# Attention and four expert layers on one core: additions to the output placed later, two tiles fetched before the hand-over

## What is computed

```
x = x + layernorm(attention(layernorm(x)))        # causal linear attention, 16 heads of 8, relu on q and k
x = x + layernorm(ffn(layernorm(x)))              # 4 layers, each:
#   logits = x @ rw[l] + rb[l]; the best 2 of 4 experts, weights renormalised
#   xhat = (x - mean) / sqrt(var + eps)
#   y_e  = gelu((xhat * g[e] + b[e]) @ w1[e] + b1[e]) @ w2[e] + b2[e]
#   x    = sum over the two experts e of weight_e * (x + y_e)
```

## Time and profile before

| | |
|---|---|
| median of 3 runs | 1578.39 us (1576.26 to 1583.17) |
| profiled execution, its own time | 1576.51 us |
| its span | 1574.6 us |
| PE, DVE, ACT, POOL busy | 88%, 78%, 71%, 54% |
| mean granted TensorE clock | 0.95 of full speed |
| attention block | up to about 403 us |
| last layer's first `fin`, last `fin` | 1312.88 us, 1559.35 us |

### The profile page before, as it was taken

The page is one execution under the profiler, slowest core; times in us unless marked ns, Lnnn a source line. Parts: engine busy times, 40 slices in busy tenths (PEclk is TensorE's granted clock), DMA queues, the critical chain, the costliest instruction groups (busy, mean ns, idle before and its releaser), DMA issues.

```text
span 1574.6 us, 36962 instructions
## 1 busy us (share of the span) xinstructions
PE 1389.8 (88%) x11037; PEld 1086.1 (69%) x11037; DVE 1233.7 (78%) x3763; ACT 1117.9 (71%) x1979; POOL 850.5 (54%) x1535
## 2 busy tenths in 40 slices
PE   6999999998679998999899999989989998888991
PEld 4666566566557877777787777778877776776770
DVE  6988788887358888788888878888887888677782
ACT  4444344442467898878788888778988788899881
POOL 2246556677665565345355534445563346787456
PEclk9998898998689999999999999999999999999995
DMA  7964565641657877665787766668766757886642
GB/s 280 400 264 137 220 245 201 232 169 31 167 163 223 250 228 212 194 180 169 211 251 227 221 184 200 180 192 262 228 214 181 213 170 199 214 206 159 178 105 21
DMA packets 181109, 314.11 MB, mean 199 GB/s; under 512 B 37568, under 2 KB 117808, under 8 KB 180528
## 3 DMA queue, kind: packets, MB, share of 16 engines
q1 hardware_dynamic: 159408, 288.27, 58.3%
q0 software_dynamic: 21504, 23.48, 6.4%
HBM read 205.20 MB, written 113.72 MB: 203 GB/s over the span
## 4 chain that ended last, share of the span: by engine, by line
PE 36%; issue 13%; DVE 12%; ACT 9%; POOL 4%; POOLq 0%; ACTq 0%; DVEq 0%
PE ps_h L1835 5%; PE ps_h L1837 5%; PE ps_h L1836 5%; PE ps_q L1868 5%; PE ps_y L1849 4%; PE ps_y L1851 4%; PE ps_y L1850 4%; ACT xh L1382 3%; ACT hh L1404 3%; DVE row L1540 2%; PE ps_t L1822 1%; DVE pbn L1483 1%; DVE hl L1477 1%; DVE row L1514 1%; POOL out_dram L1321 1%
## 5 line engine op out<-in xcount | busy, mean ns | idle before, releaser
L1398 ACT ACTIVATE hg<-ps_h,bb 128x512 f32<-128x512 f32 x592 | 387.7, 686 | 158.1 <-PE ps_h L1837 156.5
L1477 DVE TENSOR_TENSOR hl<-hg,hh 128x1024 fp32r<-128x1024 f32 x296 | 360.6, 1219 | 164.4 <-ACT hh L1404 164.3
L1404 ACT ACTIVATE hh<-hg 128x1024 fp32r<-128x1024 f32 x296 | 313.4, 1059 | 2.4
L1312 POOL DMA_INDIRECT regions<-nrow,posi x192 | 226.6, 1180 | 85.3 <-issue 47.9
L1835 PE MATMUL ps_h<-xTh,w1b 128*128 128x512 f32 x592 | 255.7, 432 | 8.4 <-ACT hg L1398 6.8
L1837 PE MATMUL ps_h<-xTh,w1b 128*128 128x512 f32 x592 | 234.9, 397 | 0.0
L1849 PE MATMUL ps_y<-hh,w2b 128*128 128x512 f32 x592 | 234.3, 396 | 0.0
L1836 PE MATMUL ps_h<-xTl,w1b 128*128 128x512 f32 x592 | 234.3, 396 | 0.0
L1851 PE MATMUL ps_y<-hh,w2b 128*128 128x512 f32 x592 | 233.3, 394 | 0.0
L1850 PE MATMUL ps_y<-hl,w2b 128*128 128x512 f32 x592 | 232.2, 392 | 0.0
L1868 PE MATMUL ps_q<-ir,yb 128*128 128x140 f32 (+2 forms) x888 | 138.8, 288 | 66.4 <-DVE base L1583 42.2
(11 more groups left out here) (280 smaller groups left out, 2630.2 us busy)
## 6 DMA issues: line engine op xcount, KB each, us to landing
w1b<-w_split SPq DMA_DIRECT2D x148, 512.0 KB, 4.1
w2b<-w_split SPq DMA_DIRECT2D x148, 512.0 KB, 4.6
regions<-zero SPq DMA_DIRECT2D x14, 4326.0 KB, 24.6
row<-regions SPq DMA_DIRECT2D x84, 294.0 KB, 4.4
w_split<-wst SPq DMA_DIRECT2D x32, 512.0 KB, 5.1
wr<-in_L_ffn_w_dram SPq DMA_DIRECT2D x32, 256.0 KB, 4.8
regions<-regions SPq DMA_DIRECT2D x24, 294.0 KB, 4.3
x<-in_L_attn_x_dram SPq DMA_DIRECT2D x16, 256.0 KB, 3.1
```

The lines of the kernel that those rows point to most:

```text
L1312: g.indirect_dma_start(out=regions[layer % 2], out_offset=bass.IndirectOffsetOnAxis(ap=posi[r % 2][:, b:b + 1], axis=0), in_=nrow[r % 2][: ...
L1398: a.activation(hg[c // 2 % PAIRS][:, c % 2 * TILE:(c % 2 + 1) * TILE], ps_h[c % BANKS][:], ACT.Gelu, bias=bb[h % BBUFS][:, c % FC:c % FC + ...
L1404: a.activation(hh[j % PAIRS][:], hg[j % PAIRS][:], ACT.Identity).then_inc(hi, 1)
L1477: v.tensor_tensor(hl[n][:], hg[n][:], hh[n][:].bitcast(F32), ALU.subtract).then_inc(lo, 1)
```

## The change

Four edits.

1. The additions of a last-layer tile get the index ENDS 2(j-10) instead of ENDS 2(j-8) in GpSimd's loop.
2. The first two operations of `last_rstd` (variance plus epsilon, mean times -1) move from GpSimd to VectorE, as `last_variance`, right behind `last_stats`.
3. The rows of the first two units are fetched by SP inside the attention block, ahead of the last tile's store of `x1`; their two buffers move to the part of memory that both blocks share.
4. Behind the barrier GpSimd does `rstd(0)` and `rstd(1)` ahead of `a_place(13)`, VectorE does `stats(0)` and `stats(1)` ahead of its wait for GpSimd's constants, and the counts of tile 14 (`count` on TensorE, `first_counts` on ScalarE) come behind PE's second chunk and ScalarE's first two gelus.

```diff
+                def first_rows():
+                    sp.wait_ge(t_tab, 1)
+                    for q in range(2):
+                        sp.wait_ge(s_scat[q], ((EARLY_FROM - 1 - q) // 2 + 1) * NB * 16)
+                    for n in range(2):
+                        at = sp.value_load(tabi[0][0:1, n, 0:1], min_val=0, max_val=ROWS - TILE)
+                        sp.dma_start(row_first[n][:], regions[0][ds(at, TILE)].rearrange("(b p) w -> p b w", p=P)).then_inc(row_in[n], 16)
                 for t in range(NT):
+                    if t == NT - 1:
+                        first_rows()
                     sp.wait_ge(a_x1, t + 1)
...
-                for n in range(2):
-                    rows_in(n)
                 for h in range(2):
                     first_weights(h)
...
                 def last_rstd(m):
                     n = PLACE[m]
-                    pool.wait_ge(f_mv, n + 1)
+                    pool.wait_ge(f_ve, 2 * n + 2)
                     wait(pool, f_n, n)
-                    g.tensor_tensor(fve[:], fmv[:, :, 1], epsc[:], ALU.add).then_inc(f_ve, 1)
-                    g.tensor_scalar(fngm[:], fmv[:, :, 0], -1.0, None, ALU.mult)
-                    pool.wait_ge(f_ve, n + 1)
                     g.tensor_tensor(frs[:], fve[:], half[:], ALU.pow).then_inc(f_rs, 1)
...
-                a_place(pool, NT - 3)
                 g.memset(oh[:, NB, :], 0.0)
...
                 pool.wait_ge(s_ir, 1)
+                rstd(0)
+                rstd(1)
+                a_place(pool, NT - 3)
                 a_choose(pool, NT - 2)
-                for n in range(3):
-                    rstd(n)
+                rstd(2)
                 a_rows_out(pool, NT - 3, range(NB))
...
+                    m = ENDS.get(2 * (j - 10))
                     if last_layer(m):
                         add_to_output(m)
                     m = ENDS.get(2 * (j - 7))
...
-                first_counts(NT - 2)
                 normed(0)
                 x_high(0)
                 normed(1)
                 gelu(0)
                 gelu(1)
+                first_counts(NT - 2)
...
+                def last_variance(m):
+                    n = PLACE[m]
+                    dve.wait_ge(f_mv, n + 1)
+                    wait(dve, f_nm, n)
+                    v.tensor_tensor(fve[:], fmv[:, :, 1], epsc[:], ALU.add).then_inc(f_ve, 1)
+                    v.tensor_scalar(fngm[:], fmv[:, :, 0], -1.0, None, ALU.mult).then_inc(f_ve, 1)
...
+                stats(0)
+                stats(1)
                 dve.wait_ge(s_ir, 1)
                 v.memset(sel[:], 0.0)
                 chained(v.tensor_scalar(tile_at[:], tiles[:, 0:LATE], float(TILE), None, ALU.mult))
-                stats(0)
-                stats(1)
                 x_rest(0)
...
                         if last_layer(n):
                             last_stats(n)
+                            last_variance(n)
...
-                pe.wait_ge(z_lu, NT)
-                count(NT - 2, a_oh)
                 x_transposes(0)
...
+                    if c == -7:
+                        pe.wait_ge(z_lu, NT)
+                        count(NT - 2, a_oh)
```

More of the change, by code:

```diff
@@ L97, in sandwich_kernel @@
         arow = [sb(f"arow{q}", [P, NB, W]) for q in range(AROWS)]
+        row_first = [sb(f"row{q}", [P, NB, W]) for q in range(2)]
         uT = sb("uT", [P, TILE])
@@ L149, in sandwich_kernel @@
         s_alone = sem("wait_alone")
+        row_in = [sem(f"row_in{q}") for q in range(ROWBUFS)]
         s_x = sem("x_in")
@@ L1017, in sandwich_kernel @@
         bb_in = [sem(f"bias_in{q}") for q in range(BBUFS)]
-        row_in = [sem(f"row_in{q}") for q in range(ROWBUFS)]
         s_moved = sem("rows_moved")
@@ L1038, in sandwich_kernel @@
             bb = [esb(f"bb{q}", [P, FC + 1]) for q in range(BBUFS)]
-            row = [esb(f"row{q}", [P, NB, W]) for q in range(ROWBUFS)]
+            row = row_first + [esb(f"row{q}", [P, NB, W]) for q in range(2, ROWBUFS)]
             nrow = [esb(f"nrow{q}", [P, NB, W]) for q in range(2)]
```

## The result

The changed kernel took 1626.34 us, the median of 3 runs (1623.51 to 1630.19), against 1578.39: 47.95 us more between the medians, and a ratio of 1.0313 on record, 95% interval 1.0275 to 1.0351. By the ratio it is 3.1% slower, where 1.9% was forecast, and 4.3 us above the end of the range. The profiled execution took 1630.19 us, with a span of 1628.4 against 1574.6.

| stretch | before | after | difference | forecast |
|---|---|---|---|---|
| start to the last operation of `x1` (end of attention) | 394.71 | 404.01 | +9.3 | 0 |
| from there to `xh` of unit 4 | 65.02 | 59.55 | -5.5 | -2.7 |
| from there to the first `fin` | 853.15 | 855.51 | +2.4 | 0 |
| first to ninth `fin` | 120.93 | 168.04 | +47.1 | +34.3 |
| ninth `fin` to the end | 140.8 | 141.3 | +0.5 | -1.5 |

The account below looks back on a forecast made before the run. ScalarE was taken to bound the last layer's eight-tile stretch (110.84 of 120.93 us busy). +34.3 (loop) - 1.5 (end) - 2.7 (hand-over) = +30.1 on 1576.51, plus 1.9 for the median: 1608.5 us, range 1590 to 1622.

Parts of the forecast that it names:

- The order, the wait and the count of periods: GpSimd's last-layer queue: rstd(n+6)'s wait for stats(n+6) comes before the additions, closing a loop; eight periods, tiles 0 to 7, +34.3 us.
- The size of a period: Last layer, one fin to the next: stats, rstd, four additions, last_rstd and hand-overs, 19.4 us against 15.1 before.
- The hand-overs: Last layer's loop: the hand-overs between engines in one period, put at 0.3 us together.
- My upper bound of a period, 20.2: Last layer's loop: 20.2 us a period if VectorE's work stretches GpSimd's operations by 0.8 us.
- Deviations: Last layer, variance and negated mean on VectorE: cost 0 in the loop, -1.5 us at the kernel's end.
- Hand-over: From the end of attention into the next block, up to xh of unit 4: -2.7 us, bounds 0 and -6.5.
- the forecast's term: Behind attention's end: GpSimd's idle 3.83 us for stats(2) goes, a wait of 1.1 us for stats(0) comes.
- its work is the same in another order: GpSimd's queue behind attention, up to rstd(4): same work, reordered, so only its idle time changes; -2.7 us.
- The faster one: Last layer: the additions leave the loop and ScalarE alone sets the pace, -10.1 us there, 1564 in all; chance 0.10.
- the absorbed one: Last layer: the stall is mostly absorbed, periods of 16 us, +7 there, 1582 in all, no change; chance 0.06.
- The granted clock: Last layer: TensorE's clock falls at each new stall and the loss isn't hidden, +14 us, 1622 and above; chance 0.06.

Follow-up runs that it names:

- The second measurement: The changed kernel run once more with nothing edited: 1617.42 us, ratio 1.0276 against the kernel before.
- the last version: The changed kernel with four fidi buffers, additions behind last_rstd (e+11) for the first eleven places and the last but one, else e+8: 1563.38 us, ratio 0.9929.

## Why the prediction was right and wrong

**The order, the wait and the count of periods: right.** The wait of `rstd(n+6)` stands in front of the additions and closes a ring through `fin(n)`. The ring shows eight times, for tiles 0 to 7, and then the spacing falls to 16.4 and 15.7. Taking the wait from its place ends it, and taking half the additions out shortens it by their length.

**The size of a period: the step that failed.** The term 8.72 + 1.67 + 7.36 + 1.31 + 0.3 = 19.4, times 8, gave 155.2 us; it measured 168.04. The missing 12.8 us are two things.
- 8 x 1.0 us: in the middle of the loop a period is 20.4. The hand-overs take 0.71 instead of 0.3, above all the 0.59 us between `pnmr` and the first addition (an addition that follows at once had 0.63 in front of it in the earlier trace rows, and I gave it no term). The additions take 7.92 instead of 7.36, since the first of them is recorded at 2.40 us. In every period it starts while VectorE runs `hl`, and it ends 1.5 to 1.6 us behind the end of that `hl` (in the rows above 1394.07 + 2.40 = 1396.47 against 1393.72 + 1.22 = 1394.94).
- 4.9 us: the first period is 22.9, the second 20.7 and the last two are 21.4 and 21.5. In the first, `pve` starts 10.8 us behind `fin` instead of 8.8 (ScalarE waits 1.90 us for PE there, and VectorE has a dozen small operations on the tables in front of `hl`), and a second addition is long too, 1.96 us. In the seventh a second addition is recorded at 2.59 us, started 0.07 us behind an `hl`; in the changed kernel's other trace that addition takes 1.55 and the period 20.38. In the eighth ScalarE has more to do (15.37 us against 13.69). The kernel before has its own excess: its spacings are 16.8 at first, 15.5 and 15.5 at the end, once 15.4 in between, and else 14.3 to 14.7. I took the mean of all eight for before, 15.1, and built the new period from a tile in the middle: excess on one side of the difference and not on the other.

My upper bound of a period, 20.2, lay below what came. It rested on a misreading: `pve`'s 0.77 us behind the additions is 0.57 more than elsewhere, not 0.8, and for 0.52 us of it (1353.47 to 1353.99) the last addition is still recorded too, so most of it is two records that overlap and no stretching by VectorE. The stretching is there, but it is on the issue of an addition.

**Deviations: right at the end, not free in the loop.** -1.3 us at the end against -1.5. In the loop I put the two operations on VectorE at 0, since they come behind `stats`. They come ahead of `hl`, and that counts. One period of the kernel with the additions moved alone, on GpSimd and on VectorE, where `fve` and `fngm` are still GpSimd's:

```profile
1388.76 2.12 POOL L1321 DMA_INDIRECT out_dram<-fin,fidi  x1 [0.58 <-issue]
```

```profile
1388.16 1.19 DVE L1478 TENSOR_TENSOR hl<-hg,hh 128x1024 fp32r<-128x1024 f32 x1
```

Here `hl` starts 0.60 us ahead of the first addition, and the addition takes 2.12 us. In the changed kernel `fve` and `fngm` stand in front of `hl`; it starts 0.35 us ahead, and the addition takes 2.40. In both the addition ends 1.53 us behind `hl`. So `last_rstd` is 0.37 us shorter (1.37 against 1.74 behind the last addition), the first addition 0.28 us longer, and 0.1 us a period is left; over the eight, with the first and the last ones, nothing (168.10 and 168.04).

**Hand-over: right direction, half the size.** Busy times from GpSimd's first operation behind the barrier to `xh` of unit 4, before and after:

```profile
403.29:459.73 56.44, 42.14 (x186) 33.03 (x186) 22.75 (x62) 35.97 (x62) 43.66 (x97) 0.83 0.74 204
```

```profile
412.55:463.56 51.01, 42.62 (x184) 33.08 (x185) 22.76 (x62) 35.60 (x63) 41.39 (x97) 0.84 0.75 209
```

-5.4 us against -2.7. GpSimd does the same 97 operations in 41.39 instead of 43.66 us, and what it does not work went from 12.8 to 9.6. The second is the forecast's term. The changed kernel's GpSimd and ScalarE there:

```profile
414.03 0.20 POOL L1278 TENSOR_TENSOR pve<-pmv,epsc 128x4 f32<-128x4 f32 x1 [1.24 <-DVE pmv L1497]
```

```profile
463.56 1.65 ACT L1391 ACTIVATE xh<-row,pnmr,prs 128x128 f32<-128x128 f32 x4 [5.20 <-POOL pnmr L1283]
```

The wait for `stats(0)` is 1.24 us where 1.1 was expected, and the idle 3.83 us in front of `rstd(2)` went. That "its work is the same in another order" holds for the operations and not for their time, which fell by 2.3 us. The 12 issues of rows (15.3 us before, 13.3 now) have most of it. What runs beside them has changed, but what makes them shorter was not taken apart.

**The rivals.** The faster one and the absorbed one are refuted: `stats` came 8.7 us behind `fin`, as read. The granted clock did fall in each period: PE sits idle 6.15 us, and the matmuls behind it take 0.63 us instead of 0.39 for 3.4 us. By the Trainium skill ("TensorE: Matmul & The Clock Gate", section "HAM oscillation — how this bites in real kernels") such a loop starts cold in each turn; the trace agrees, with the 0.83 of the period. But `pmv` was ready 8.68 us behind `fin` all the same, and by the 8.76 us at either clock the cost was nothing.

**Why the time fell out of the range.** Without attention, the spans are 1179.9 and 1181.0 us in the two traces of before and 1224.4 and 1223.1 in the two of the change: +42 to +45 us. The second measurement has +43.5 (38.5 to 48.7), the additions alone +45.1. The first has +49.4 by its ratio (43.4 to 55.4). With the right period the forecast had been near 1620, inside the range, so the period alone did not carry the time out of it. The traced execution (1630.19 us) had 9.3 us more of attention than that of before, for which the range had no term; the other two, 1623.51 and 1626.34, have no trace, and why they too lie above 1622 stays open.

## What to carry to other kernels

An operation on an in-order queue is never moved alone: write the queue out in its new order and look which wait now stands in front of it. If that wait hangs on the consumer of what stands behind, the loop is closed, and its length is the sum over the ring; one place in front of or behind `rstd`, in the same turn of the loop, was worth some 50 us here. When the difference of a period is worked out, take both sides from the same tiles, the first and last ones by themselves. An operation that is moved to an engine with time to spare still shifts what stands behind it there; look at what that meets. And a buffer's reuse is safe to put at nothing only where its wait stands behind the landing, which comes some microseconds behind the end of the issue; a step in a schedule belongs where the queue has a gap.

## What the runs showed of the hardware

- An indirect addition's issue on GpSimd takes 1.53 to 1.7 us, and up to 2.6 where VectorE is running an operation with two inputs in SBUF when it starts. In the five traces read for this (before, changed, additions alone, additions behind `last_rstd`, the last version) every addition over 1.7 us starts under such an operation and ends 1.4 to 1.6 us behind its end. It is `hl` in most cases, and `row` from `joined` and `row` in the tail (from 1593.01 for 0.74 us in the changed kernel, with an addition from 1593.15 for 2.12). An `hl` that starts later than the addition does not lengthen it: beside the addition of 1.65 us at 1346.81 lies the whole of

```profile
1346.94 1.23 DVE L1477 TENSOR_TENSOR hl<-hg,hh 128x1024 fp32r<-128x1024 f32 x1 [2.84 <-ACT hh L1404]
```

The Trainium skill ("GPSIMD Engine Reference", section "Specifications") has GpSimd's SBUF interfaces shared with VectorE, with contention when VectorE has two SBUF inputs; the traces agree where such an operation is already running, and show none of it where the operation starts later. This is by order in time and not by an experiment made for it.
- Between an operation of GpSimd and the first indirect addition behind it lie 0.58 us in the periods shown (0.63 in the earlier trace rows), between additions 0.30.
- Additions landed so that the wait was released 3.23 us behind the end of the last issue in the round shown, and 4.9 in the longest wait of that kernel.
- One unchanged program's attention took from 387.3 to 404.0 us in two executions, at granted clocks of 0.90 and 0.81 in one 50 us stretch of it. In other kernels that clock and the end of attention do not go together (0.83 and 389.1, 0.86 and 398.8).
